# Place matrices with the node tile innermost, edge lists kept in SBUF, and the store of x's rows waited for one stage later

## What is computed

```python
def gt_layer(x, src, dst, ntype, etype, ...):
    k, q, v = typed_linear(x, ntype, Wk), typed_linear(x, ntype, Wq), typed_linear(x, ntype, Wv)
    kw = rel_apply(k[src], etype, Watt)                  # one of 8 relations for each edge
    a = (kw * q[dst]).sum(-1) * pri[:, etype].T / SQRT_D
    alpha = softmax of a over the edges of one dst
    m = rel_apply(v[src], etype, Wmsg)
    agg = segment_sum(alpha * m, dst)
    out = silu(typed_linear(agg, ntype, Wa))
    al = sigmoid(skip[ntype])
    return layernorm(out * al + x * (1 - al)) * g + b

h = relu(layernorm(x))
emb = two gt_layers over h
out = x + emb @ Wff + bff
```

## Time and profile before

| | us |
|---|---|
| median of 3 runs | 2797.17 |
| lowest and highest run | 2794.03, 2850.97 |
| profiled execution, first to last instruction | 2852.2 |
| DVE busy in it | 2349.6 (82%) |
| POOL busy in it | 2024.0 (71%) |
| PE busy in it | 1755.6 (62%) |
| ACT busy in it | 1285.3 (45%) |

### The profile page before, as it was taken

How to read it: one execution, slowest core, us unless ns; L and a number is a source line. 1 busy time by engine, 2 the same in 40 slices (tenths; PEclk the granted TensorE clock), 3 DMA queues, 4 the chain that set the end, 5 groups by cost and what they waited for, 6 DMA issues and landing times. The chain is left out here.

```text
span 2852.2 us, 49119 instructions
## 1 busy us (share of the span) xinstructions
PE 1755.6 (62%) x11035; PEld 1547.8 (54%) x11035; DVE 2349.6 (82%) x5622; ACT 1285.3 (45%) x4592; POOL 2024.0 (71%) x2030
## 2 busy tenths in 40 slices
PE   1925745665666666666677745666666666666566
PEld 1824535555556555555555535665565666655444
DVE  6935758888888888888778758888888888888588
ACT  0005743444444444444567714444444444444555
POOL 2885667777777777777377677777777777777276
PEclk8558986777777777777679968777767776677655
DMA  5326986666666666666357776666666666666311
GB/s 132 26 62 253 358 287 195 184 185 184 185 185 183 185 183 183 182 182 184 96 198 280 287 229 183 183 183 183 182 184 188 183 182 182 184 185 171 123 47 37
DMA packets 386053, 512.90 MB, mean 180 GB/s; under 512 B 74933, under 2 KB 297835, under 8 KB 373268
## 3 DMA queue, kind: packets, MB, share of 16 engines
q0 software_dynamic: 101952, 328.62, 36.8%
q1 hardware_dynamic: 274712, 179.39, 21.5%
q10 hardware_dynamic: 9104, 1.86, 0.4%
HBM read 382.63 MB, written 142.96 MB: 184 GB/s over the span
## 5 line engine op out<-in xcount | busy, mean ns | idle before, releaser
L1248 POOL DMA_INDIRECT g_rows<-node_kv,edge_key_sb x1564 | 1486.5, 950 | 483.2 <-issue 465.1
L1428 ACT ACTIVATE acc<-g_ps_sum 128x127 f32 x1564 | 414.4, 265 | 679.9 <-DVE g_gained L1360 546.4
L1489 PE MATMUL g_ps_q<-g_qw,g_hot_t 128*128 128x128 f32 x3128 | 623.2, 360 | 54.3 <-DMA g_qw<-node_q 54.3
L1489 PEld LDWEIGHTS g_ps_q<-g_qw,g_hot_t 128*128 128x128 f32 x3128 | 580.1, 273 | 60.6 <-DMA g_qw<-node_q 55.5
L1432 ACT ACTIVATE acc<-acc,g_gained,g_scale x1564 | 600.0, 384 | 2.2 <-issue 1.2
L1478 PE MATMUL g_ps_sum<-g_hot,g_rows 128*128 128x128 f32 x3128 | 585.1, 355 | 0.8 <-ACT acc L1432 0.8
L1478 PEld LDWEIGHTS g_ps_sum<-g_hot,g_rows 128*128 128x128 f32 x3128 | 562.2, 272 | 1.1 <-ACT acc L1432 1.0
L1282 DVE TENSOR_TENSOR g_rows<-g_rows,g_ps_q 128x512 f32<-128x512 f32 (+1 forms) x446 | 264.2, 610 | 144.9 <-DMA g_rows<-node_kv,edge_key_sb 115.9
L1512 PE MATMUL g_ps_a<-g_ends,head_of_row 112*8 112x56 f32 x224 | 34.6, 247 | 498.9 <-DVE g_alpha L1317 498.9
L1512 PEld LDWEIGHTS g_ps_a<-g_ends,head_of_row 112*8 112x8 f32 x224 | 13.6, 88 | 517.1 <-issue 517.1
L1445 ACT ACTIVATE g_exp_t<-g_shifted 112x128 f32<-112x128 f32 x112 | 34.7, 309 | 431.6 <-DVE g_shifted L1301 431.6
(11 more groups left out here) (249 smaller groups left out, 2928.2 us busy)
## 6 DMA issues: line engine op xcount, KB each, us to landing
g_qw<-node_q SPq DMA_DIRECT2D x1564, 64.0 KB
g_rank_row<-edge_rank SPq DMA_DIRECT2D x110, 448.0 KB
g_rows<-node_kv,edge_key_sb POOLq DMA_INDIRECT x1564
node_agg<-n_agg SPq DMA_DIRECT2D x24, 256.0 KB, 2.3
node_rows<-node_x SPq DMA_DIRECT2D x2, 1792.0 KB
node_q<-l_blank_q SPq DMA_DIRECT2D x1, 3200.0 KB
node_q<-n_q_sb,node_slot POOLq DMA_INDIRECT x112, 4.3
node_kv<-n_kv,node_id POOLq DMA_INDIRECT x112
```

Source lines behind the costliest of these rows:

```text
L1248: g_.indirect_dma_start(out=rows[b % U][:, g, :], out_offset=None, in_=scratch["kv"][:, :], in_offset=bass.IndirectOffsetOnAxis(ap=tab["ke ...
L1428: a.activation(acc[:, bass.ds(w + 1, P - 1)], ps_sum[q % BANKS][:, n, 1:P], ACT.Copy).then_inc(s["copied"], 1)
L1489: ins = t.matmul(ps_q[q % BANKS][:, n, :], hot_t[b % 2][:, g, :], qw[b % 2][:, g, :], start=True, stop=True)
```

## The change

The matrices `at_place` and `in_tile` are stored with the node tile as the last axis, and so are the two products made from `in_tile`. `place_lo` and `place_hi` become bf16. The row 0 to 127 repeated for every node tile (`row_rep`, 128 x 50 elements in each partition) is written by GpSimd ahead of its clearing of `node_x`, in place of VectorE's `row_b`, and VectorE waits for it ahead of L250. TensorE takes the columns of one tile with a step of 50 elements. The three edge lists live in tensors that last from `edge_lists` to the end of `edge_tables`; the loads of L498 to L500 and VectorE's wait for them go, and the sort's branch loads the three lists at its end. The two stores of x's rows count on a semaphore of their own, and SyncE waits for it in the first node stage.

```diff
-        dsts, srcs, rels, prev = (sb(f"l_{n}", [Q, W], I32) for n in ("dst", "src", "rel", "prev"))
+        dsts, srcs, prev = tab["edge_dst"], tab["edge_key"], tab["edge_prev"]
+        rels = sb("l_rel", [Q, W], I32)
...
-        place_lo = sb("l_place_lo", [P, NT])
-        place_hi = sb("l_place_hi", [P, NT])
+        place_lo = sb("l_place_lo", [P, NT], BF16)
+        place_hi = sb("l_place_hi", [P, NT], BF16)
+        row_rep = sb("l_row_rep", [P, P, NT], BF16)
...
-        numbers = sb("l_numbers", [P, NT, 2, TT], BF16)
+        numbers = sb("l_numbers", [P, 2, TT, NT], BF16)
...
-                then(v.tensor_copy(tab["row_b"][:, :], c["row"][:, :]))
...
-                then(v.tensor_tensor(tab["at_place"][:, :, :], tab["row_b"][:, :].rearrange("p (o e) -> p o e", o=1).to_broadcast([P, NT, P]),
-                                     place_lo[:, :].rearrange("p (t o) -> p t o", o=1).to_broadcast([P, NT, P]), ALU.is_equal))
-                then(v.tensor_tensor(tab["in_tile"][:, :, :], tab["row_b"][:, 0:TT].rearrange("p (o e) -> p o e", o=1).to_broadcast([P, NT, TT]),
-                                     place_hi[:, :].rearrange("p (t o) -> p t o", o=1).to_broadcast([P, NT, TT]), ALU.is_equal))
+                dve.wait_ge(s["row_rep"], 1)
+                then(v.tensor_tensor(tab["at_place"][:, :, :], row_rep[:, :, :],
+                                     place_lo[:, :].rearrange("p (o t) -> p o t", o=1).to_broadcast([P, P, NT]), ALU.is_equal))
+                then(v.tensor_tensor(tab["in_tile"][:, :, :], row_rep[:, 0:TT, :],
+                                     place_hi[:, :].rearrange("p (o t) -> p o t", o=1).to_broadcast([P, TT, NT]), ALU.is_equal))
...
-                    then(v.tensor_tensor(numbers[:, :, n, :], tab["in_tile"][:, :, :],
-                                         a[:, :].rearrange("p (t o) -> p t o", o=1).to_broadcast([P, NT, TT]), ALU.mult))
+                    then(v.tensor_tensor(numbers[:, n, :, :], tab["in_tile"][:, :, :],
+                                         a[:, :].rearrange("p (o t) -> p o t", o=1).to_broadcast([P, TT, NT]), ALU.mult))
...
-                    ins = t.matmul(ps_id[:, 0:2 * TT], tab["at_place"][:, i, :], numbers[:, i, :, :].rearrange("p a t -> p (a t)"),
+                    ins = t.matmul(ps_id[:, 0:2 * TT], tab["at_place"][:, :, i], numbers[:, :, :, i].rearrange("p a t -> p (a t)"),
...
+                nc.gpsimd.tensor_copy(row_rep[:, :, :], c["row"][:, :].rearrange("p (e o) -> p e o", o=1).to_broadcast([P, P, NT])).then_inc(s["row_rep"], 1)
                 nc.gpsimd.memset(tab["x"][:, :, :], 0.0)
...
-        cur, prev, key, lo_i, hi_i = (sb(f"e_{n}", [Q, W], I32) for n in ("cur", "prev", "key", "lo_i", "hi_i"))
+        cur, prev, key = tab["edge_dst"], tab["edge_prev"], tab["edge_key"]
...
-                sp.dma_start(cur[:, :], edge_dst[1:EP + 1].rearrange("(p w) -> p w", w=W)).then_inc(s["loaded"], 16)
-                sp.dma_start(prev[:, :], edge_dst[0:EP].rearrange("(p w) -> p w", w=W)).then_inc(s["loaded"], 16)
-                sp.dma_start(key[:, :], edge_key.rearrange("(p w) -> p w", w=W)).then_inc(s["loaded"], 16)
...
-                    sp.dma_start(scratch["rows"][n * TL * P:(n + 1) * TL * P, :].rearrange("(t p) d -> p t d", p=P), tab["x"][:, part, :]).then_inc(s["stored"], 16)
-                sp.wait_ge(s["stored"], 112 + 16 * LOADS)
+                    sp.dma_start(scratch["rows"][n * TL * P:(n + 1) * TL * P, :].rearrange("(t p) d -> p t d", p=P), tab["x"][:, part, :]).then_inc(c["x_rows_out"], 16)
...
-                dve.wait_ge(s["loaded"], 48)
...
-                    v.tensor_tensor(slots[:, :, k, :], tab["in_tile"][:, :, :],
-                                    a[:, :].rearrange("p (t o) -> p t o", o=1).to_broadcast([P, NT, TT]), ALU.mult).then_inc(s["slots"], 1)
+                    v.tensor_tensor(slots[:, k, :, :], tab["in_tile"][:, :, :],
+                                    a[:, :].rearrange("p (o t) -> p o t", o=1).to_broadcast([P, TT, NT]), ALU.mult).then_inc(s["slots"], 1)
...
                 spent.clear(sp)
+                if first:
+                    sp.wait_ge(c["x_rows_out"], 16 * 2)
...
-        tab["at_place"] = places.enter_context(nc.sbuf_tensor("at_place", [P, NT, P], BF16))
-        tab["in_tile"] = places.enter_context(nc.sbuf_tensor("in_tile", [P, NT, TT], BF16))
+        tab["at_place"] = places.enter_context(nc.sbuf_tensor("at_place", [P, P, NT], BF16))
+        tab["in_tile"] = places.enter_context(nc.sbuf_tensor("in_tile", [P, TT, NT], BF16))
+        for name in ("dst", "key", "prev"):
+            tab[f"edge_{name}"] = places.enter_context(nc.sbuf_tensor(f"edge_{name}_rows", [Q, W], I32))
```

## The result

The changed kernel takes 2807.3 us (median of 6 runs) against 2796.94 of before (6 runs beside them): a ratio of 1.0032, 95% interval 1.0021 to 1.0044, or 8.9 us longer (5.9 to 12.3); the two medians differ by 10.4, and what follows goes by the ratio. So the rows shown ahead are set beside a second profile, of the unchanged kernel in an execution of ordinary length (`e_before` under the experiments, span 2791.3 us). The profiled execution of the changed kernel has a span of 2799.0 us.

The account below looks back on a forecast made before the run. It took the preparation's three parts as ended by VectorE (ScalarE next), GpSimd's gathers and SyncE's store wait. Gains 4.3 + 6.2 + 2.3 + 7.3 = 20.1 us from the median 2797.17 gave 2777 us, range 2765 to 2800.

Parts of the forecast that it names:

- The execution it was read from: Preparation terms read from a profiled execution of 2852.2 us; the same 20.1 us subtracted from the median 2797.17.
- (d): End of the tables stage: SyncE's wait for the second x store goes; gain 7.3 us, bounds 0 and 7.3.
- (c): Slots of the tables stage: faster products of 2800 hold GpSimd's gathers for less time; gain 2.3 us.
- TensorE's step: In edge_lists, 50 matmuls reading operands with a step of 100 bytes: 5.15 us instead of 4.78, 0.4 us more.
- (a): Place matrices in edge_lists: faster VectorE compares and products, less added costs; gain 4.3 us, between -3.8 and 4.6.
- the bound of 44.82: End of edge_lists: ScalarE's DMA issue ends at 44.82 us, so only 4.61 of 7.69 us are gained.
- (b): Start of the tables stage: lists kept in SBUF, VectorE starts at 51.20 instead of 57.40 us; gain 6.2 us.
- The stages behind: Open case: something larger in the edge and node stages behind the preparation; chance 0.06.
- a slow copy: Rival in edge_lists: GpSimd's copy takes 14.5 us, (a) gives -3.8 instead of 4.3; 2785 us, chance 0.15.
- an unhidden store: Rival at the tables stage's end: store not hidden or another end replaces SyncE's wait; gain 12.8, 2784 us, chance 0.08.
- slow products: Rival in the preparation: VectorE's products keep their old rate; 10.1 us gained, 2787 us, chance 0.05.
- the one on the far side: Rival, slower than before: a very slow GpSimd copy holds VectorE's casts; 2811 us at a 40 us copy, chance 0.04.

Follow-up runs that it names:

- e_undo_d: The changed kernel with SyncE again waiting for the two stores of x's rows at the end of the tables stage; 2803.12 us, ratio to before 1.0023.
- x_columns: Against x_dve_rep, at_place back in the old layout; only in_tile and its products keep the node tile innermost; 2792.93 us, ratio to before 0.9988.
- x_dve_rep: The changed kernel with the repeated row written by VectorE instead of GpSimd; 2792.4 us, ratio to before 0.9986.
- x_weights: Against x_dve_rep, only at_place keeps the node tile innermost; in_tile and its products have the old layout; 2788.93 us, ratio to before 0.9967.
- e_undo_a: The changed kernel with the place matrices as before and no GpSimd copy; lists in SBUF and later store wait kept; 2788.88 us, ratio to before 0.9977.

## Why the prediction was wrong

It said 2777.0 us, 20 less than before, with 2765 to 2800 as its range; the time went the other way, to 2807.3. "Within 2%" was right. By its own steps:

**The execution it was read from.** The prediction noted that the profiled execution was 2.0% longer than the median, and went on: "as the terms are waits and instructions of the preparation, I subtract the same 20.1 from the median". This step failed. The 55 us that the execution was longer lay for the most part in that very preparation, and could have been found in the rows: 45 gathers behind the compares at 1.3 us each are 59 us. A kernel whose other runs are 55 us shorter can hardly have them there. With the gathers among the compares, GpSimd doesn't set the end of the tables stage. So term (d), 7.3 us, was nothing in an ordinary execution (the store lands 24 us ahead of the end; `e_undo_d` differs by 0.1%, not told from zero). And term (c), priced at a gain of 2.3 through held gathers, had another size and sign: VectorE's products and TensorE's sum are themselves the path there.

**TensorE's step.** "264 one-hot matmuls in 27.17 us, gives 0.103 us each, or 5.15 for 50 ... I take that: 0.4 us more." This is the term that was mis-sized: it measured 10.76 us, 5.98 more than the row of before. The row that priced it, shows VectorE's pace and not TensorE's: 14 matmuls belong to one pair of compares, 14 x 0.103 is 1.44 us, and in the change the pairs start 1.44 us apart as well, at TensorE's double clock. Whatever the step costs there is hidden behind VectorE. The same matmuls in the tables stage got no price at all, since gathers covered them in the execution that was read: from 3.96 to 10.70, which with its waits is 6.7 us lost for the 2.9 that the products gained. The Trainium skill's rule on lines of 16 bytes, named above, would have spoken for a loss.

**Part (a).** The compares and products were right to 0.01 us (3.49 and 1.62). The copy took 5.52 (6 was taken) and the type cast was held, as foreseen from the earlier trace rows: it ran from 8.28 to 15.43, until copy and memset were both over at 15.35 (15.9 was foreseen). What followed was 1.74 us late (15.86 against 14.12), not 3.0, as the key update (L219) was over together with the cast instead of behind it; against `e_before`, where the copy of the types starts at 13.33, it was 2.5 us. The Trainium skill's "SBUF — State Buffer", "Who interferes with whom", agrees in that the cast was held; the release between the two instructions, which by that rule alone would have come at 9.8 us (9.3 with the copy's measured 5.52), did not happen here. ScalarE's last issue ended at 42.80 us, so the bound of 44.82 that the prediction put on the gain was not what ended the part: TensorE was. 7.7 us won on VectorE, 1.7 lost to the hold and 6.0 to TensorE leave nothing, where 4.3 were foreseen (against `e_before` the part ends 0.7 us later); the bounds, -3.8 to 4.6, held.

**Part (b).** Right: VectorE starts with the stage at 51.25 (57.40 before), the loop at 68.49 (74.83), and by the experiments the lists are worth 6.4 to 7 us, where 6.2 were foreseen. No gather was lost to the compares.

**The stages behind.** "0.06 for something larger in the stages behind" was the only place for what cost most: 10.9 us by 7 ns on each of 1564 gathers. This term was put near nothing and measured 10.9. No row of before shows a copy on GpSimd, so its effect could not be priced from there. What could be read is the lever: two stages of 1000 us that go at GpSimd's pace turn each nanosecond on their gathers into 1.6 us. The rivals that the prediction named (a slow copy, an unhidden store, slow products) did not occur, and neither did the one on the far side.

With the measured sizes the sum comes out: (a) 0, (b) -6.4 to -7, (c) 6.7 - 2.9 = +3.8, (d) 0, gathers +10.9, together +7.7 to +8.3 us against 8.9 (5.9 to 12.3) measured.

## What to carry to other kernels

When the profiled execution is longer than the other runs by more than their spread, first find the stretch that holds the excess, and price no term inside it from that profile alone. A row gives the cost of an instruction only where its engine is the one that sets the pace; for a layout change, ask for each reader of the tensor which operand takes the step, since here weights read it at no cost that shows and moving columns at more than twice the time. And ask of any instruction added to an engine how many instructions that engine runs later on the path, because a few nanoseconds on each can outweigh all that is visible in the block that was edited.

## What the runs showed of the hardware

- One executed copy with a cast on GpSimd, of 128 or of 819200 elements, made the later gathers of the edge stages longer, 942 to 949 ns at the shortest; the cause is open. It is no general slowing: the indirect writes of the last stage (L1120, L1127 in the change) went from a mean of 1048 ns in `e_before` to 1041.
- The same gather among the same compares took 77.43 us in one execution of the unchanged kernel and 1.34 us in another. What decides between the two is open, and no run here tries it.
- TensorE's granted clock stood at 1.00 (2.4 GHz) from 51 to 171 us in the change, and at 0.50 to 0.58 (0.50 is 1.2 GHz) from 51 to 174 us in the unchanged kernel, behind 50 matmuls that lasted 10.76 us in the one and 4.85 in the other. From 74 to 148 us `x_columns` and `x_dve_rep`, with 10.48 and 10.76, show 1.00 too, `x_weights` and `e_undo_a`, with 4.64 and 4.85, 0.50. In the change it bought nothing: the one-hot loop took 80.6 and 80.5 us, since VectorE sets its pace, and the stepped matmuls at the higher clock were still the slower ones.
